# Plain float32 operands for the first product of the 128-slot expert blocks

## The reference

```
x = x + tanh(g_xattn[l]) * xattn_l(layernorm(x), ctx)
x = x + tanh(g_ffn[l])   * ffn_l(layernorm(x))
# ffn of the first layer: 8 experts, each token goes to its two best
h   = gelu(einsum('nd,edf->enf', xf, W1) + b1)      # 256 -> 1024
y   = einsum('enf,efd->end', h, W2) + b2            # 1024 -> 256
out = einsum('ne,end->nd', comb, y)
```

## Time and profile before

| what | value |
|---|---|
| median of 3 runs | 836.87 us (836.34 to 839.56) |
| the profiled execution | 837.54 us |
| its span in the trace | 835.7 us |
| PE busy, share of the span | 749.6 us, 90% |
| DVE busy | 609.0 us, 73% |
| ACT busy | 477.5 us, 57% |
| POOL busy | 385.7 us, 46% |
| first layer's experts in the trace | about 241 to 491 us |

### The profile page before, as it was taken

How to read it: one execution, slowest core, us unless ns; L and a number is a source line. 1 busy time by engine, 2 the same in 40 slices (tenths; PEclk the granted TensorE clock), 3 DMA queues, 4 the chain that set the end, 5 groups by cost and what they waited for, 6 DMA issues and landing times. The chain is left out here.

```text
span 835.7 us, 17408 instructions
## 1 busy us (share of the span) xinstructions
PE 749.6 (90%) x6872; PEld 634.1 (76%) x6872; DVE 609.0 (73%) x1212; ACT 477.5 (57%) x722; POOL 385.7 (46%) x379
## 2 busy tenths in 40 slices
PE   6999999999469999999999947999999998459995
PEld 6666767667459999999999946666676667359995
DVE  4777777753759998998998925777777752869982
ACT  3377666753057776776776623576666653526640
POOL 6465554112145666666666235565442112083532
PEclk9999999999669999999999989999999999569998
DMA  7001000010286888888788327000000000477732
GB/s 230 20 20 40 26 28 19 11 53 26 78 305 195 262 253 259 255 255 260 239 243 265 100 32 228 14 14 28 15 15 14 15 15 26 154 257 250 215 86 29
DMA packets 45521, 101.35 MB, mean 121 GB/s; under 512 B 9824, under 2 KB 36064, under 8 KB 37760
## 3 DMA queue, kind: packets, MB, share of 16 engines
q0 software_dynamic: 16800, 65.46, 26.4%
q1 hardware_dynamic: 28640, 34.78, 12.7%
HBM read 84.22 MB, written 15.74 MB: 120 GB/s over the span
## 5 line engine op out<-in xcount | busy, mean ns | idle before, releaser
L600 DVE TENSOR_REDUCE mx_a<-ps_max_a 128x2 f32<-128x512 f32 x256 | 164.1, 684 | 39.7 <-PE ps_max_a L846 38.6
L89 PE MATMUL ps_h_e<-xe_t_e,w_e 128*128 128x256 f32 (+1 forms) x480 | 137.6, 287 | 10.7 <-DVE xe_t_e L1770 10.7
L452 ACT ACTIVATE prob_a<-ps_st_a 128x2048 f32<-128x2048 f32 x64 | 120.1, 1877 | 29.0 <-PE ps_st_a L865 28.7
L91 PE MATMUL ps_h_e<-xe_t_e,w_e 128*128 128x256 f32 (+1 forms) x480 | 134.5, 280 | 0.0
L90 PE MATMUL ps_h_e<-xe_t_e,w_e 128*128 128x256 f32 (+1 forms) x480 | 134.4, 280 | 0.0
L89 PE MATMUL ps_y_e<-w_e,h_e 128*128 128x256 f32 x424 | 118.4, 279 | 0.0
L90 PE MATMUL ps_y_e<-w_e,h_e 128*128 128x256 f32 x424 | 117.9, 278 | 0.0
L91 PE MATMUL ps_y_e<-w_e,h_e 128*128 128x256 f32 x424 | 117.9, 278 | 0.0
L89 PEld LDWEIGHTS ps_h_e<-xe_t_e,w_e 128*128 128x128 f32 x480 | 92.7, 193 | 13.2 <-DVE xe_t_e L1770 13.1
L90 PEld LDWEIGHTS ps_h_e<-xe_t_e,w_e 128*128 128x128 f32 x480 | 92.2, 192 | 0.0
L91 PEld LDWEIGHTS ps_h_e<-xe_t_e,w_e 128*128 128x128 f32 x480 | 92.1, 192 | 0.0
(11 more groups left out here) (234 smaller groups left out, 1767.1 us busy)
## 6 DMA issues: line engine op xcount, KB each, us to landing
w_raw_w<-L_w SPq DMA_DIRECT2D x14, 1024.0 KB, 6.0
ctx_raw_a<-ctx_t SPq DMA_DIRECT2D x16, 256.0 KB, 4.7
normalised_weighted<-xr SPq DMA_DIRECT2D x16, 256.0 KB, 2.2
x_sb<-x SPq DMA_DIRECT2D x8, 256.0 KB, 4.6
x_sb<-x SPq DMA_DIRECT2D x2, 1024.0 KB, 8.6
x<-x_sb SPq DMA_DIRECT2D x8, 256.0 KB, 2.6
out<-x_sb SPq DMA_DIRECT2D x4, 512.0 KB, 7.6
q_s_a<-m_t_a SPq DMA_DIRECT2D x64, 4.0 KB
```

The source lines that it names most:

```text
L89: pe.matmul(out, lhs[0], rhs[0], start=start, stop=False)
L91: return pe.matmul(out, lhs[0], rhs[1], start=False, stop=stop)
L452: act.activation(prob[n % 2][:, :, :, :], ps_st[:, :, :, :], ACT.Exp, scale=HD ** -0.5).then_inc(prob_ready, 1)
L600: dve.tensor_reduce(mx[:, q, h:h + HG + 1:HG], ps_max[j][:, :, :], AX.X, ALU.max).then_inc(max_done, 1)
```

## The change

The small blocks of the first layer no longer split the operands of their first product. The inputs' transposed copy goes to a plain float32 tile of its own (`xe_plain`), W1 is gathered into the first 2056 words of `more` (raised from 1920 words to hold it) with a semaphore of its own (`small_ld`), and TensorE multiplies the raw W1 with `xe_plain` in one plain float32 matmul where there were three of float32r. For a small block, ScalarE's copies of W1 and VectorE's low parts of W1 and of the inputs go away; the bias copy stays and now waits for the gather on VectorE. The full blocks keep the two `w1_raw` buffers for themselves, by a count of full blocks (`splits`) instead of the block's parity. The gather of a small block's W1 waits until the first product of the small block before it is done. The second product is as it was.

```diff
-MORE = 1920
+MORE = 2056
@@ expert_phase
+    if layer == 0:
+        xe_plain = sb("xe_plain", [P, KC, P])
+        small_ld = sem("small_ld")
+    more = sb("more", [P, MORE])
@@
+    def small(b):
+        return order[b][2] == 1
+    def splits(b):
+        return sum(not small(c) for c in range(b))
+    fulls = [c for c in range(blocks) if not small(c)]
+    def earlier_small(b):
+        return max([c + 1 for c in range(b) if small(c)], default=0)
+    def w1_home(b):
+        return more[:, 0:KC * F + FC] if small(b) else w1_raw[splits(b) % 2]
+    def w1_landed(b):
+        return small_ld if small(b) else w1_ld[splits(b) % 2]
+    def w1_loads(b):
+        return 16 * (b - splits(b) + 1) if small(b) else 16 * (splits(b) // 2 + 1)
@@ GpSimd
         def load_w1(b):
-            if b < blocks:
-                pool.wait_ge(w1_ready, b - 1)
-                gather_weights(pool, "w1", buffers, shared, dram, b)
+            if b >= blocks:
+                return
+            if small(b):
+                wait(pool, h_ps, earlier_small(b) * NP)
+            else:
+                pool.wait_ge(w1_ready, fulls[splits(b) - 2] + 1)
+            c = order[b][0]
+            pool.indirect_dma_start(out=w1_home(b)[:, :], out_offset=None, in_=dram["w1"],
+                                    in_offset=bass.IndirectOffsetOnAxis(ap=shared["block_row"][:, c:c + 1], axis=0)
+                                    ).then_inc(w1_landed(b), 16)
@@ ScalarE
         def w1_high(b, k):
+            if small(b):
+                return
...
         def inputs_high(b):
             act.wait_ge(xe_ps, b + 1)
-            w = order[b][2] * P
-            act.activation(xe_t[b % 2][0][:, :, 0:w], ps_x[b % 2][:, :, 0:w], ACT.Copy).then_inc(xe_hi, 1)
+            if small(b):
+                wait(act, h_ps, earlier_small(b) * NP)
+                act.activation(xe_plain[:, :, :], ps_x[b % 2][:, :, 0:P], ACT.Copy).then_inc(xe_hi, 1)
+            else:
+                act.activation(xe_t[b % 2][0][:, :, :], ps_x[b % 2][:, :, :], ACT.Copy).then_inc(xe_hi, 1)
@@ VectorE
+        def small_bias(b):
+            dve.wait_ge(small_ld, w1_loads(b))
+            wait(dve, hid_ready, (b - 1) * NP)
+            dve.tensor_copy(b1[b % 2][:, :], w1_home(b)[:, KC * F:KC * F + FC]).then_inc(w1_ready, 1)
         def w1_low(b, k):
-            dve.wait_ge(w1_hi, b * KC + k + 1)
+            if small(b):
+                if k == KC - 1:
+                    small_bias(b)
+                return
+            dve.wait_ge(w1_hi, splits(b) * KC + k + 1)
...
-            dve.tensor_tensor(xe_t[b % 2][1][:, :, 0:n * P], ps_x[b % 2][:, :, 0:n * P], xe_t[b % 2][0][:, :, 0:n * P].bitcast(F32),
-                              ALU.subtract).then_inc(xe_ready, 1)
+            if not small(b):
+                ins = dve.tensor_tensor(xe_t[b % 2][1][:, :, :], ps_x[b % 2][:, :, :], xe_t[b % 2][0][:, :, :].bitcast(F32),
+                                        ALU.subtract)
+            ins.then_inc(xe_ready, 1)
@@ TensorE, first_product
                 for j in range(2):
                     for k in range(KC):
+                        if small(b):
+                            ins = pe.matmul(ps_h[jp % RB][:, j, 0:w],
+                                            w1_home(b)[:, k * F + (2 * jp + j) * P:k * F + (2 * jp + j + 1) * P],
+                                            xe_plain[:, k, :], start=k == 0, stop=k == KC - 1)
+                            continue
                         ins = split_matmul(...)
```

More of the change, by code:

```diff
@@ L1529, in expert_phase @@
     listed, comb_stored = sem("listed"), sem("comb_stored")
-    tiles = {"more": sb("more", [P, MORE]), "later": hid + y + xe, "ps_h": ps_h, "ps_y": ps_y, "listed": listed, "comb_stored": comb_stored}
+    tiles = {"more": more, "later": hid + y + xe, "ps_h": ps_h, "ps_y": ps_y, "listed": listed, "comb_stored": comb_stored}
     def sync_part(sp):
@@ L1625, in w1_high @@
         def w1_high(b, k):
+            if small(b):
+                return
             if k == 0:
-                act.wait_ge(w1_ld[b % 2], loaded(b))
+                act.wait_ge(w1_landed(b), w1_loads(b))
                 wait(act, h_ps, (b - 1) * NP)
-            act.activation(w1[b % 2][0][:, k, :, :], w1_raw[b % 2][:, k * F:(k + 1) * F].rearrange("p (j f) -> p j f", j=FC),
+            act.activation(w1[b % 2][0][:, k, :, :], w1_home(b)[:, k * F:(k + 1) * F].rearrange("p (j f) -> p j f", j=FC),
                            ACT.Copy).then_inc(w1_hi, 1)
@@ L1698, in dve_part @@
     def dve_part(dve):
+        def small_bias(b):
+            dve.wait_ge(small_ld, w1_loads(b))
+            wait(dve, hid_ready, (b - 1) * NP)
+            dve.tensor_copy(b1[b % 2][:, :], w1_home(b)[:, KC * F:KC * F + FC]).then_inc(w1_ready, 1)
         def w1_low(b, k):
-            dve.wait_ge(w1_hi, b * KC + k + 1)
+            if small(b):
[3 more added lines that the diff above has]
+            dve.wait_ge(w1_hi, splits(b) * KC + k + 1)
             ins = dve.tensor_tensor(w1[b % 2][1][:, k, :, :],
-                                    w1_raw[b % 2][:, k * F:(k + 1) * F].rearrange("p (j f) -> p j f", j=FC),
+                                    w1_home(b)[:, k * F:(k + 1) * F].rearrange("p (j f) -> p j f", j=FC),
                                     w1[b % 2][0][:, k, :, :].bitcast(F32), ALU.subtract)
@@ L1705, in w1_low @@
                 if layer == 0:
-                    ins = dve.tensor_copy(b1[b % 2][:, :], w1_raw[b % 2][:, KC * F:KC * F + FC])
+                    ins = dve.tensor_copy(b1[b % 2][:, :], w1_home(b)[:, KC * F:KC * F + FC])
                 ins.then_inc(w1_ready, 1)
@@ L1768, in inputs_low @@
                 dve.wait_ge(picked, b + 1)
-                dve.tensor_reduce(slot_weight[:, b, 0:n], by_expert[:, 0:n, :], AX.X, ALU.add)
-            dve.tensor_tensor(xe_t[b % 2][1][:, :, 0:n * P], ps_x[b % 2][:, :, 0:n * P], xe_t[b % 2][0][:, :, 0:n * P].bitcast(F32),
-                              ALU.subtract).then_inc(xe_ready, 1)
+                ins = dve.tensor_reduce(slot_weight[:, b, 0:n], by_expert[:, 0:n, :], AX.X, ALU.add)
+            if not small(b):
+                ins = dve.tensor_tensor(xe_t[b % 2][1][:, :, :], ps_x[b % 2][:, :, :], xe_t[b % 2][0][:, :, :].bitcast(F32),
+                                        ALU.subtract)
+            ins.then_inc(xe_ready, 1)
         for b in range(2):
```

## The result

The changed kernel takes 827.51 us in the median of 4 runs (827.27 to 830.11), the one before beside it 837.32 (4 runs): a ratio of 0.9886, 95% interval 0.9858 to 0.9915, or 9.8 us less. The prediction was 826.0, range 823 to 831. The profiled execution takes 827.27 us with a span of 825.5.

What follows compares the result with a forecast made beforehand. TensorE was taken as the bound, VectorE 5% behind. Gains of 1.40 us (first small block), 5 x 1.58 and 1.58 (last) sum to 10.9 us: 836.9 - 10.9 = 826.0 us, with 80% from 823 to 831 us.

Steps and rivals of the forecast that it cites:

- Two records for a plain product: Small block's first product on TensorE: 16 plain products, two records each, make 32 records in place of 48.
- The price of one, 0.118 us: Plain 128-column record on TensorE: 0.118 us, so 32 take 3.78 us, 1.58 us less in every small block.
- VectorE shrinks ahead of a small block, and the wait for ScalarE takes the first part: Period ahead of a small block: VectorE from 10.30 to 8.84 us; wait at the first cast grows by 1.1 us.
- The small period has nothing to spare at 1.63 us: Small period: VectorE ends at 10.08, TensorE at 10.13 us; of a gain of 1.63 or more, VectorE keeps the rest.
- a wait of over 0.5 us in this place: Sign of being wrong: TensorE waits over 0.5 us for the inputs in the full period behind a small block.
- The lag falls to 0.20: End of the period ahead of a small block: VectorE's lag behind TensorE falls from 1.03 to 0.20 us.
- the rival of the gain given back a period later: VectorE's period ahead of small blocks doesn't shrink, TensorE waits one period later: gain 6.4 us, 830.5 us; chance 0.08.
- Costs nothing: ScalarE's fewer copies, waits of gathers and `inputs_high`, and the bias copy behind its gather (some 13 us later) hold nothing up.
- The slower rival: Each plain product loads weights four times: 1.79 us more per small block, 12.5 us in all, 849.4 us; chance 0.05.

Runs made afterwards that it cites:

- e5: Changed kernel, but the plain product of a small block moves its 128 columns twice, 256 in a record: 849.43 us, ratio 1.0127 to the kernel before.
- e4: Changed kernel, but the plain product of a small block moves only 64 of its 128 columns: 828.27 us, ratio 0.9889 to the kernel before.
- e1: Changed kernel, but VectorE still makes the low parts of W1 and inputs for small blocks, unread: 833.65 us, ratio 0.9953 to the kernel before.
- e2: Changed kernel, but every second plain product of a small block is issued twice, giving 48 records: 837.05 us, ratio 0.9997 to the kernel before.
- e8: Changed kernel, but W1's home and semaphores go back to the block's parity, in the old buffers: 842.69 us, ratio 1.0039 to the kernel before.
- e7: Changed kernel, but the first layer's full blocks are plain too, without splits of W1 or inputs: 856.19 us, ratio 1.0198 to the kernel before.

## Why the prediction was right

*Two records for a plain product*: right, 32 in a small block. *The price of one, 0.118 us*: the term that was mis-sized. It is 3.49 / 32 = 0.109 us (from 345.23 to 349.19, less 0.47 for the transposes), and the product gives 1.87 us in a small block, not 1.58. The prediction put 128 plain columns level with 256 of float32r, which is right for the streaming (e5). But 256 columns at full clock stream in 107 ns, so the 0.119 of those records isn't their streaming either, and the plain ones follow as closely as float32r ones with 128 columns. e4 and e5 show the two limits.

*VectorE shrinks ahead of a small block, and the wait for ScalarE takes the first part*: right. From `y_raw` to `y_raw` it is 376.05 - 366.63 - 0.54 = 8.88 us (8.84 forecast), with a wait of 1.30 us at the first cast. *The small period has nothing to spare at 1.63 us*: right in kind, and it decided the sum. With 1.87 us TensorE was 0.21 us faster than VectorE's 9.85, and this came back in the period behind. The chain there was also 0.13 us longer than forecast: from `y_raw` to the end of the inputs' low part it is 363.64 + 0.68 - 355.28 = 9.04 us, not 8.91. So 0.41 + 9.04 + 0.05 = 9.50 us, where the prediction had 9.16 and named a wait of over 0.5 us in this place as a sign of being wrong: it is 0.51 to 0.58 us (0.88 behind block 3), and that sign came true.

Of the 13.0 us that the small periods gave, 2.1 went in the six periods behind small blocks (0.52 behind block 3, about 0.3 behind the others). Some 0.7 went in the other full periods, which mostly last 11.43 to 11.48 us where they alternated between about 11.3 and 11.53 us before (11.53 in the earlier trace rows, 11.27 for block 15), and 0.2 in the time to block 2. Why the same records lay closer in every second cycle before is not shown. The longer periods are there too with VectorE's load back (e1), with 48 records (e2) and with W1 in the old buffers (e8), so none of these alone sets them. 10.0 us are left, against 10.9 forecast. That the sum came so near is luck in part: there are two errors of opposite sign, 2 us from the record's price and nearly 3 from what came back.

*The lag falls to 0.20*: right, and e1 shows that 6 us of the gain hang on it: without it, the rival of the gain given back a period later is what happens, at 833.65 where it was put at 830.5. *Costs nothing*: right, none of the seven bias copies waited for its gather. The new home was counted as free; e8 shows that it is a condition of the change and no detail: in the old buffers the changed kernel is 3.7 us slower than the one before.

The slower rival, four weight loads for a plain product, is out: the trace has 224 weight loads for the 112 plain products of the small blocks, two for each, and 32 records take 3.49 us. The Trainium skill, "FP8 and Floating Point Precision", section "TensorE Precision Notes", counts four passes through the array for true float32. In the columns the trace agrees with it (e5: two records for a product, and each takes about two cycles for a column), in the weight loads it has two and not four.

## What to carry to other kernels

Here a plain float32 record cost 0.109 to 0.111 us with 64 or 128 moving columns, as much as a float32r one with 128 (0.112), so a plain product of two records (0.22 us) beat a split of three (0.34). With 256 columns it was the other way, 0.43 us (2 x 0.216) against about 0.35. When two engines are within 5% of each other, as here, ask with what lag the second ends each period: only the part of the first engine's gain that left this lag at its floor passed on. What came back could be had by moving the one result that was waited for ahead of work that nobody waited for. Before a gathered buffer is held longer, look at what is queued behind its next gather.

## What the runs showed of the hardware

TensorE's clock fell to its lower level behind waits of 1.97 us (e1), 1.92 and 1.99 us (e8). It also fell behind 5.78 us in e7 (0.50 from 260 to 262 us). In e1 the lower clock cost 13.30 - 11.68 = 1.6 us on top of the wait. Behind the waits of 0.5 to 0.9 us between the blocks of the changed kernel the clock stayed at 1.00, and so it did behind those of 1.3 to 1.4 us of e1 and up to 1.65 us of e8. But it also stayed at 1.00 behind the 2.67 us of e7, so the length of a wait alone doesn't say whether the clock falls; what else decides isn't shown. Where it fell, a wait of 2 us cost nearly twice its length. That is a part of what e1 and e8 took beyond what was reckoned; in e8 the more frequent waits are the other.
